# Attention scores by head in row tiles, mixed over heads by a second matmul, in a talking-heads attention block on one core

## The reference

```
xn   = group_norm(x, 32 groups)
q, k = conv1x1_bn(xn)   # 8 heads x 32 channels each
v4   = conv1x1_bn(xn)   # 1024 channels;  vl = bn(depthwise_conv3x3(v4))
attn = einsum('bhid,bhjd->bhij', q, k) * SCALE + ab[:, BIAS_IDXS]
attn = einsum('bhij,gh->bgij', attn, th1w) + th1b      # first mix over heads
attn = softmax(attn, axis=-1)
attn = einsum('bhij,gh->bgij', attn, th2w) + th2b      # second mix over heads
o    = relu(einsum('bhij,bhjd->bhid', attn, v) + vl)
y    = x + conv1x1_bn(o)                               # projection, 1024 -> 384
```

## Time and profile before

| | |
|---|---|
| time, median of 3 runs | 4535.93 us (4534.8 to 4536.65) |
| the profiled execution | 4534.58 us, its span 4532.8 us |
| granted TensorE clock over the span | 0.999 |
| PE busy | 4505.5 us, 99% |
| DVE, ACT, POOL busy | 93%, 79%, 30% |
| DMA | 356 MB, 79 GB/s, queues 27.3% of 16 engines' span |

### The profile page before, as it was taken

The page is one execution under the profiler, slowest core; times in us unless marked ns, Lnnn a source line. Parts: engine busy times, 40 slices in busy tenths (PEclk is TensorE's granted clock), DMA queues, the critical chain, the costliest instruction groups (busy, mean ns, idle before and its releaser), DMA issues.

```text
span 4532.8 us, 108461 instructions
## 1 busy us (share of the span) xinstructions
PE 4505.5 (99%) x33666; PEld 4502.5 (99%) x33666; DVE 4197.4 (93%) x10015; ACT 3570.3 (79%) x8508; POOL 1360.9 (30%) x1288
## 2 busy tenths in 40 slices
PE   7999999999999999999999999999999999999999
PEld 7999999999999999999999999999999999999999
DVE  8999999999999999999999999999999999999998
ACT  7787877878778787787787877878778778787786
POOL 2323323323233232332322323323233232332322
PEclk9999999999999999999999999999999999999999
DMA  3322222223222232222322322223222232232222
GB/s 94 97 65 81 86 69 87 65 81 92 70 81 74 72 97 65 81 82 68 93 65 81 88 72 82 68 78 97 65 81 79 67 97 65 81 86 68 88 65 76
DMA packets 211502, 356.05 MB, mean 79 GB/s; under 512 B 15843, under 2 KB 132691, under 8 KB 211413
## 3 DMA queue, kind: packets, MB, share of 16 engines
q1 hardware_dynamic: 211478, 355.75, 27.3%
HBM read 199.71 MB, written 155.98 MB: 78 GB/s over the span
## 4 chain that ended last, share of the span: by engine, by line
PE 99%; DMA 0%; POOL 0%; DVE 0%; SPq 0%; ACT 0%; issue 0%; POOLq 0%; DVEq 0%
PE psA L293 45%; PE psA L426 15%; PE psL L293 13%; PE psM L293 10%; PE psM L404 9%; PE psL L404 7%; PE psA L306 0%; DMA qa<-in_wqkv 0%; SPq L254 0%; POOL xs L822 0%; DVE probs L730 0%; DMA by_key<-probs 0%; POOL wp_lo L863 0%; DVE q_lo L722 0%; ACT w_hi L443 0%
## 5 line engine op out<-in xcount | busy, mean ns | idle before, releaser
L700 DVE SCALAR_TENSOR_TENSOR psC<-vpad,par,psC 128x406 f32<-128x406 f32 x3072 | 1807.2, 635 | 0.0
L584 ACT ACTIVATE probs<-probs,nmax 112x196 f32<-112x196 f32 x1792 | 803.2, 451 | 128.8 <-DVE nmax L759 112.9
L293 PE MATMUL psA<-x_hi,w_lo 128*128 128x392 f32 x2304 | 794.9, 345 | 6.0 <-DVE x_lo L679 6.0
L293 PE MATMUL psA<-x_hi,w_hi 128*128 128x392 f32 x2304 | 785.7, 341 | 0.0
L293 PE MATMUL psA<-x_lo,w_hi 128*128 128x392 f32 x2304 | 785.1, 341 | 0.0
L426 PE MATMUL psA<-qa,shared 105*128 105x196 f32 x4096 | 690.9, 329 | 0.0
L426 PEld LDWEIGHTS psA<-qa,shared 105*128 105x128 f32 x4096 | 677.2, 190 | 0.4 <-DVE shared L794 0.3
L857 POOL TENSOR_TENSOR k_lo<-qk,k_hi 128x392 fp32r<-128x392 f32 x128 | 159.9, 1249 | 1636.4 <-ACT k_hi L490 1636.4
L722 DVE SCALAR_TENSOR_TENSOR q_lo<-qk,th,q_hi 128x392 fp32r<-128x392 f32 x1024 | 618.3, 632 | 2.0 <-ACT q_hi L486 1.9
L486 ACT ACTIVATE q_hi<-qk,th 128x392 fp32r<-128x392 f32 x1024 | 594.5, 618 | 2.1
L461 ACT ACTIVATE o_hi<-shared 128x392 fp32r<-128x392 f32 x512 | 271.6, 530 | 391.3 <-DVE shared L794 391.3
(11 more groups left out here) (85 smaller groups left out, 10723.1 us busy)
## 6 DMA issues: line engine op xcount, KB each, us to landing
by_key<-probs SPq DMA_DIRECT2D x512, 224.0 KB, 3.6
qa<-by_key SPq DMA_DIRECT2D x128, 448.0 KB, 4.3
qk<-by_key SPq DMA_DIRECT2D x128, 448.0 KB, 6.9
xs<-in_x SPq DMA_DIRECT2D x64, 588.0 KB, 3.8
shared<-in_x SPq DMA_DIRECT2D x64, 588.0 KB, 3.8
out<-shared SPq DMA_DIRECT2D x63, 588.0 KB, 3.0
qa<-in_wqkv SPq DMA_DIRECT2D x3, 768.0 KB, 7.1
stage_wp<-in_wp SPq DMA_DIRECT2D x1, 1536.0 KB, 9.6
```

The costliest lines, as they stand in the source:

```text
L293: last = nc.tensor.matmul(dst, w, r, start=(begin and n == 0), stop=(end and n == 2))
L584: nc.scalar.activation(row, row, ACT.Exp, bias=nmax[:, img, b:b + 1], scale=-1.0, accum_out=rowsum[:, img, b:b + 1]).then_inc(s_exp, 1)
L700: nc.vector.scalar_tensor_tensor(a if tap == 7 else sums, src, taps[:, c, TAPS[tap]:TAPS[tap] + 1], a if tap == 0 else sums, MUL, ADD).the ...
```

## The change

The scores are computed for each source head by itself, and the first mix becomes a matmul of its own.

Scores by head: a unit is 7 query rows with all 14 columns of one image (98 queries), so there are 4 units a pair. For a unit, PE does 8 matmuls in float32 (`head_scores`), one for each head, each contracting over that head's 32 channels, with 98 queries stationary and 196 keys moving; the four heads of a channel half lie on partitions 0, 32, 64 and 96 and write to four PSUM banks. The unit's matmuls stand behind value tiles 2 to 5. ACT and DVE copy the scores to `scores` in `qa`, two banks each, and SP moves them by 8 DMAs a unit, SBUF to SBUF, to `by_head`, whose partitions are (column, head).

The mix: 14 float32 matmuls of 392 columns with the 112 x 112 matrix `kron1` give the same banks as before. Projection tiles 0, 1 and 2 now stand behind the fourth, eighth and twelfth of them. The splits of q and k go away. `turned` moves from `probs` to `qa`, with one turn per image behind the fourth and eighth mixing matmul; POOL takes half of `head_major` and six of the eight `low`; ACT's relu also writes back to `acc`; AV goes through the units with the images alternating and starts when all 14 copies of mixed attention are done. The diff, cut:

```diff
+        heads_at = VT // 2 * ACC
+        by_head = shared[0:HP, heads_at:heads_at + 2 * RES * PIX].rearrange("p (i n) -> p i n", i=2)
...
+        scores = qa[0:UNIT, :].rearrange("p (i c h n) -> p i c h n", i=2, c=2, h=NH)
+        turned = qa[:, 0:TURNED].rearrange("p (i b c n) -> p i b c n", i=2, b=BLOCKS, c=VT)
...
+        def score_bank(r):
+
+            return (psL if r < 2 else psM)[:, r % 2, 0:2 * PIX]
+
+        UNITS = [(img, c) for img in range(2) for c in range(2)]
...
+            def moves(t, u):
+
+                img, c = UNITS[u]
+                sp.wait_ge(s_score_a, 8 * t + 2 * u + 2)
+                sp.wait_ge(s_score_v, 8 * t + 2 * u + 2)
+                cols = slice(c * UNIT * RES, (c + 1) * UNIT * RES)
+                for h in range(NH):
+                    sp.dma_start(by_head[h::NH, img, cols].rearrange("w (b j) -> w b j", b=ROWS_B),
+                                 scores[0:UNIT, img, c, h, :]).then_inc(s_moved[u], 16)
...
+            def keys_in(t, img):
+
+                if img == 0:
+                    sp.wait_ge(s_moved[2], MOVES * (t + 1))
+                    wait_alone(sp, s_moved[3], MOVES * (t + 1))
+                sp.wait_ge(s_vt_out[img], OUTS * (t + 1))
+                for jc in range(2):
+                    sp.dma_start(raw[img][0:ROWS, jc, :],
+                                 by_key[img, jc * HALF:jc * HALF + ROWS, :]).then_inc(s_raw[img], 16)
...
+                    wait_alone(sp, s_olo, 6 * t)
+                    wait_alone(sp, s_olo_v, 2 * t)
+                    wait_alone(sp, s_av_mm, 8 * t)
+                for u in range(4):
+                    moves(t, u)
+                turned_out(t, 0)
+                turned_out(t, 1)
+                keys_in(t, 0)
+                keys_in(t, 1)
                 if not first:
...
+            def head_scores(t, first, u):
+
+                img, c = UNITS[u]
+                if u:
+                    pe.wait_ge(s_score_a, 8 * t + 2 * u)
+                    pe.wait_ge(s_score_v, 8 * t + 2 * u)
+                else:
+                    pe.wait_ge(s_qk_sb, 4 * t + 4)
+                    if not first:
+                        pe.wait_ge(s_mix_sb, 14 * t)
+                at_ = (2 * img + c) * UNIT
+                for kt in range(QT):
+                    for r in range(QUADS):
+                        part_ = slice(r * KD, (r + 1) * KD)
+                        mm = nc.tensor.matmul(score_bank(r)[0:UNIT, kt * PIX:(kt + 1) * PIX],
+                                              q[part_, kt, at_:at_ + UNIT],
+                                              k[part_, kt, img * PIX:(img + 1) * PIX], start=True, stop=True)
+                mm.then_inc(s_score_mm, 1)
...
+                    if m < 6:
+                        head_scores(t, first, m - 2)
...
-                else:
-                    project(t, 0, True)
-                    project(t, 1, True)
-
-                pe.wait_ge(s_klo, 2 * (t + 1))
-                pe.wait_ge(s_qlo, 16 * (t + 1))
+
                 for n in range(RES):
                     img, b0 = n // 7, 2 * (n % 7)
+                    if n == 0:
+                        pe.wait_ge(s_score_a, 8 * t + 8)
+                        pe.wait_ge(s_score_v, 8 * t + 8)
+                    if n % 7 == 0:
+                        pe.wait_ge(s_moved[2 * img], MOVES * (t + 1))
+                    if n % 7 == 3:
+                        pe.wait_ge(s_moved[2 * img + 1], MOVES * (t + 1))
                     if n >= 4:
                         pe.wait_ge(s_score, 28 * t + 2 * n - 6)
-                    elif not first:
-                        pe.wait_ge(s_mix_sb, 14 * (t - 1) + 11 + n)
-                    for b in (b0, b0 + 1):
-                        for kt in range(QT):
-                            px = slice(img * PIX, (img + 1) * PIX)
-                            mm = split3(logit_bank(n)[:, (b - b0) * PIX:(b - b0 + 1) * PIX],
-                                        q_lo[:, img * RES + b, kt, :], q_hi[:, img * RES + b, kt, :],
-                                        k_lo[:, kt, px], k_hi[:, kt, px], kt == 0, kt == QT - 1)
-                    mm.then_inc(s_logit_mm, 1)
+                    nc.tensor.matmul(logit_bank(n)[:, 0:2 * PIX], kron1[:, :, :].rearrange("p g i -> p (g i)"),
+                                     by_head[:, img, b0 * PIX:(b0 + 2) * PIX], start=True, stop=True
+                                     ).then_inc(s_logit_mm, 1)
                     if n == 2 and not last:
-                        if not first:
-                            pe.wait_ge(s_pout, 3 * (t - 1) + 2)
+                        pe.wait_ge(s_v_sb, VT * (t + 1))
                         pe.wait_ge(s_stat, 4 * (t + 1))
                         group_sums(t + 1)
-
-                if not first:
-                    project(t, 2, True)
-
...
-                    pe.wait_ge(s_vt_sb, 4 * t + 2 * img + 2)
-                    pe.wait_ge(s_mix_sb, 14 * t + 7 * img + 7)
...
+                    pe.wait_ge(s_vt_sb[img], 2 * (t + 1))
+                pe.wait_ge(s_mix_sb, 14 * t + 14)
+                for u in range(8):
+                    n, img = divmod(u, 2)
+                    if u >= 2:
...
+                nc.scalar.activation(o_hi[:, 2 * n:2 * n + 2, img * PIX:(img + 1) * PIX], a, ACT.Relu).then_inc(s_relu, 1)
+                nc.scalar.activation(a, a, ACT.Relu).then_inc(s_relu, 1)
...
+                for u in range(4):
+                    values(2 + u)
+                    score_copy(t, u, 0)
+                    score_copy(t, u, 1)
+                    if u in (1, 2):
+                        conv_centre(t, first, u + 1)
+                    elif not last:
+                        stat(t + 1, 0, u // 3)
+                for m in (6, 7):
+                    values(m)
+                    if not last:
+                        stat(t + 1, 1, m - 6)
                 if first:
...
+                CENTRES = {8: 4, 11: 5, 23: 6, 25: 7}
...
+                    if n in (7, 15) and not first:
+                        projected(t, n // 8)
                 if not first:
                     projected(t, 2)
-                COPIES = {1: (0, 0), 3: (0, 1), 10: (1, 0), 13: (1, 1)}
                 for use, (img, n) in enumerate(USES):
                     act.wait_ge(s_mix_mm, 14 * t + use + 1)
-                    if use == 0 and not first:
-                        act.wait_ge(s_av_mm, 8 * t)
+                    if use == 0:
+                        act.wait_ge(s_vt_out[0], OUTS * (t + 1))
+                        act.wait_ge(s_vt_out[1], OUTS * (t + 1))
+                        act.wait_ge(s_moved[2], MOVES * (t + 1))
                     if use == 7:
-                        act.wait_ge(s_vt_sb, 4 * t + 2)
+                        act.wait_ge(s_moved[3], MOVES * (t + 1))
+                        act.wait_ge(s_vt_sb[0], 2 * (t + 1))
                     src = mix_bank(use)[:, 0:4 * HP].rearrange("p (j g m) -> p j g m", j=2, g=NH)
                     nc.scalar.copy(attn[:, img, :, :, 2 * n * RES:(2 * n + 2) * RES], src).then_inc(s_mix_sb, 1)
-                    if use in COPIES:
-                        head_major(t, *COPIES[use])
-                    if use == 6 and not last:
+                    if use in (3, 6):
+                        head_major(t, use // 4)
+                if not first:
+                    act.wait_ge(s_proj_mm, 3 * t)
+                for u in range(8):
+                    relu(t, u)
+                    if u == 0 and not last:
                         act.wait_ge(s_v_mm, VT * (t + 1))
                         x_high(t + 1)
...
+                def score_copies(u):
+                    img, c = UNITS[u]
+                    dve.wait_ge(s_score_mm, 4 * t + u + 1)
+                    for r in (2, 3):
+                        nc.vector.tensor_copy(scores[0:UNIT, img, c, r:NH:QUADS, :],
+                                              score_bank(r)[0:UNIT, :].rearrange("p (k n) -> p k n", k=QT)
+                                              ).then_inc(s_score_v, 1)
+
+                def turn(img):
+                    dve.wait_ge(s_v_sb, VT * (t + 1))
+                    for u in (img, img + 1):
+                        dve.wait_ge(s_moved[u], MOVES * (t + 1))
+                    at_ = PITCH + 1 + img * PITCH * PITCH
+                    nc.vector.transpose(turned[:, img, :, :, :].rearrange("p b c n -> p c b n"),
+                                        vpad[:, :, at_:at_ + BLOCKS * BLK].rearrange("p c (b n) -> p c b n", b=BLOCKS)
+                                        ).then_inc(s_turned, 1)
...
+                convs(14)
+                if first:
+                    dve.wait_ge(s_wlo, CT)
+                for u in range(4):
+                    score_copies(u)
+                    convs(2 if u < 3 else 3)
...
+                    if n in (3, 7):
+                        turn(n // 4)
+                        convs(3)
+                    if n == 11:
+                        convs(7)
...
```

(30 more changed lines are left out.)

303 lines of the change are left out of this document (105 added, 198 removed).

## The result

| | before | after |
|---|---|---|
| time, median | 4535.68 us (4534.8 to 4536.65) | 5048.72 us (5043.28 to 5050.53) |
| ratio, 95% interval | 1 | 1.1129 (1.111 to 1.1148) |
| mean granted TensorE clock | 0.999 | 0.968 |
| TensorE busy | 99% | 90% |
| one pair | 70.26 us | 78.82 us in the pair read here |

A forecast was written before the change was run, and what follows sets the result against it. The prediction took PE, 99% busy at 70.26 us a pair, as the bound. PE work -0.4 us plus stalls 1.6 gave +1.2 us a pair, x 63 = +78: 4614 us, range 4420 to 4780.

The forecast's parts named there:

- Scores, 1.49 us a unit: PE's head scores: 16 instructions a unit in 9 slots of 0.166 us, 1.49 us, between full and no overlap.
- the reason from program order: Head scores: a matmul's second instruction waits for its first and, in program order, holds up the next row group.
- The scaled weight loads: Head scores: weight loads, 0.11 us apart for 128 columns, scaled to 0.084, one at a time: 1.35 us a unit.
- Rival A: Head scores: the four row groups overlap fully, 0.66 us a unit; 4400 to 4465 us; chance 0.18.
- Mixing matmul, 0.658 us: First mix on PE: each float32 matmul of 392 columns takes 0.658 us, 14 of them 9.2 us a pair.
- Switching, 0.14 seven times: PE loses 0.14 us at each score unit and each mixing group before a projection tile: 1.0 us a pair.
- Use 4: Second mixing: PE waits for ACT's copy of mixed attention, wanted at 51.7 and done at 52.3; stall 0.6 us.
- Start of AV: AV waits for all 14 copies of mixed attention, the last behind the last matmul; stall 0.8 us.
- Next value tile: Next pair's tile 0 waits for unit 6's add, behind two convolution instructions on DVE; 0.2 to 0.3 us late.
- The moves, costed at nothing: SP's 8 DMAs a unit take 3.0 to 3.7 us and land in time for PE, with cover of 4 us or more.
- POOL's queue: POOL's copies at 2.3 us each leave image 1's mixing weights ready before use 7; cover 1.6 us.
- Rival C: POOL's chain makes PE wait at use 7 through slow copies or late `raw[0]`; 4700 to 4930 us; chance 0.13.

The follow-up runs named there:

- experiment 6: Kernel of experiment 4 with the loop over row groups outermost, so one row group's four instructions stand one after the other: 4622.26 us, ratio 1.0192.
- experiments 7: Kernel of experiment 5; AV's first unit waits for image 0 only, projection 2 behind mixing matmul 13, two convolution instructions before AV: 4395.34 us, ratio 0.9691.
- experiment 8: Kernel of experiments 7 with five of DVE's seven convolutions moved from behind the rows of mixing matmul 11 to behind those of 13: 4351.89 us, ratio 0.9595.
- experiment 4: Changed kernel with POOL issuing four of the eight moves of each unit, all data moved: 4620.76 us, ratio 1.0187.
- experiment 5: Kernel of experiment 4 with convolution centres 2 and 3 one unit earlier on ACT, behind units 0 and 1: 4485.58 us, ratio 0.989.

## Why the prediction was wrong, step by step

**What bounds the kernel.** Right: that an edit pays by what it takes from PE as long as no new wait appears. The result is that condition failing.

**Scores, 1.49 us a unit.** Wrong, on the dear side, so the error spoke against the change. Measured 1.05 with its switching, against 1.49 + 0.14. The step that failed is the reason from program order: neither a matmul's second instruction nor the loop order holds up another row group (experiment 6). The scaled weight loads, the second reason, rested on loads for the whole height of the array and were no bound either, since 16 of them fit into 0.85 us. Rival A, the full overlap, is what happened on TensorE; the estimate from the Trainium skill's figure (TensorE: Matmul & The Clock Gate, part 3), 0.86 us, was nearly the 0.85 from first start to next tile.

**Mixing matmul, 0.658 us.** Right: 0.66.

**Switching, 0.14 seven times.** A misreading of the earlier trace rows. The record of the first matmul behind AV starts at 2056.14, before AV's instructions are through: AV starts at 2045.65, and 64 x 0.166 later is 2056.28. One more matmul of 0.178 gives 2056.46, which is where the second one starts. Nothing is lost there, nor in front of a projection tile; around a unit 0.2 is lost, which is in the 1.05. PE's work came out at 67.2 us instead of 69.9; the gain of the change was 3.1 us a pair instead of 0.4.

**The stalls named.** Use 4: 0.6 forecast, 0.67 in the pair by the view and 0.92 from start to start. Start of AV: 0.8 forecast, 0.62 and 0.79. Next value tile: 0.2 to 0.3 forecast, 0.32 and 0.68. All three were found where they were said to be and for the reasons given, and experiments 7 and 8 took each away. Their sum, 2.4 us from start to start, is above the 1.6 forecast and inside its 0.8 to 2.5.

**The stall not named.** The fourth unit, 1.6 us a pair. The prediction counted DVE's and ScalarE's work in the head scores' stretch as sums ("ACT then has 2.15 us of work for a unit and tile") and didn't follow the two queues through each other: ScalarE's centre behind its copies, DVE's convolution behind that centre, DVE's copies behind that convolution.

**The moves, costed at nothing: the failing step.** "A unit is 615 KB: 3.0 us at that rate, 3.7 if it goes by packets". That took the price of a unit from the transfer rate of eight DMAs that were held up by their transfers. For a unit it is 8 x 0.845 = 6.8 us, while the DMA engines are at 0.30. The text had nearly the right number beside it (0.79 us each, the fourth unit landing at 41). That was luck: an issue of those DMAs takes anything from 0.33 to 1.13 us in the trace of the kernel before, growing from the first to the fourth, while a move takes 0.80 with SP's queue full or nearly empty. It asked with it only whether TensorE's mixing matmuls would be in time. They nearly were: 1.6 us of waiting. The next paragraph says that the turned values stand behind all 32 moves, but starts them at 39, the end of turn 1, and doesn't carry the 41 over. The turned values could go at 41.2 us of the pair instead of 39 and are read back behind that; `raw[0]` landed at 56.5 against the 47.5 of the prediction. Of these 9 us, 2.2 are the later start; about 2.4 come from the four writes of image 0, which were to be out long before and now stand in the same row of eight (6.3 us); and 4.4 are the landing, 8.7 us from the first issue of the read-back against the 4.3 of the earlier trace rows (the median of the page after is 6.3 for one). Why it lands later wasn't tried, but it isn't the moves on SP's queue: in experiment 4 SP begins the read-back 42.3 us into the pair and POOL's copies begin at 50.8, 8.4 us later, and there TensorE doesn't wait at use 7. So the late landing alone is covered, and the 4.6 us of the queue are what broke the cover.

**POOL's queue.** The cover was larger than forecast, since `head_major` takes 1.0 us a copy on POOL, not 2.3. With it the chain had 4 us to spare (47.5 + 2.0 + 1.0 = 50.5 against 54.7). It was overrun by 9 us of lateness, while TensorE itself came to use 7 1.4 us later than forecast (56.1). Rival C was the right place, the wait for `mixw` at use 7, with 2 to 5 us a pair against 3.76; its price was given for the wrong cause (slow copies), and its chance, 0.13, was too low, since it counted the landing only up to 3 us late.

**The clock.** The text named "a granted clock under 1.00 in any stage" as what would break every term. It did: after 3.76 us of idle TensorE the clock is 0.50 for 3.41 us, 1.2 GHz instead of 2.4. Over the run that adds 162 us to 475 of waits, a third on top. The kernel of experiment 8 has the same matmuls and a clock of 0.998, so it is the idle stretches and not the matmuls over 32 rows that lower it. No term of the sum and no rival had it, and so even rival C, at 4700 to 4930, ended below what was measured.

In short: +78 us forecast, +513 measured. TensorE's work is 3.1 us a pair cheaper (-198 in the run, where the forecast had -25); waits for SP's queue +265, fourth unit +103, the named stalls +106 (+100 forecast), all by the view; clock +157 against the kernel before. That makes +433. The other 80 us are, by estimate, what the view leaves out of the waits: 1.4 us in the pair read here, 90 us in 64 such pairs.

## What to carry to other kernels

- Cost a DMA twice: by its bytes on the DMA engines, and by its issue on the queue that sends it. Many small ones (32 of 75 KB here) fill the issuing queue while the DMA engines are busy at only 0.30. Then read who stands behind them on that queue, not only who waits for them.
- A wait removed while a later one sets the end is given back there (about 15 us are left); the same edit behind the repaired queue gave 135 us. So test the edits of a slower kernel together with the largest cause before dropping them: the change as made was 11% slower, and with its issues shared between two engines and four waits gone it is 4% faster.
- Read the price of a switch from the starts on both sides of it. The recorded start of one instruction can lie before the work ahead of it is done, and then the distance to the next start looks like a loss (0.14 us in the earlier trace rows, and 0.30 us in front of the projection tile read above, both nothing).
- Where two engines feed each other inside a loop, follow both queues through one turn. A sum of their work finds no wait of this kind.

## What the runs showed of the hardware that was not expected

- Eight float32 matmuls over 32 rows each, 16 instructions, start four at a time, read as one from each row group, 0.17 to 0.22 us from wave to wave, whatever their program order. One 196-column instruction alone takes 0.166, so a wave of four costs little more than one instruction alone.
- The issue of an SBUF to SBUF DMA on SP takes 0.80 us (98 rows, 14 partitions by 7), 0.76 (98 rows, plain), 0.76 with twice the bytes, 0.595 with 96 rows (one run), and 0.80 also when only four are issued in a pair; on POOL 0.593 (98 rows).
- Going between float32 and float32r instructions over the whole height of the array costs nothing: 4 mixing matmuls and one projection matmul take 2013.90 to 2016.74, 2.84 us, against 4 x 0.66 + 0.178 = 2.82. Going into and out of the 32-row matmuls costs about 0.1 us each.
- In the pair shown, after 3.76 us of idle TensorE the granted clock was 0.50 for 3.41 us; with no repeated wait above 1.6 us (experiment 4) the mean clock of the run was 0.992, and with none above 0.9 (experiment 5) 0.999.
